# New places for the pieces of layer 0's front in a pass of a Mamba and mixture-of-experts kernel

## The chip, the cores and the metric

One Trainium2 chip, one core. The metric is the device time of one execution in microseconds. The program ran three times; the number to predict is the median of such runs for the changed kernel.

## The reference, cut to what matters

Two layers stand one after the other. The change lies in layer 0, which adds a Mamba block and a mixture of eight experts to its input (8192 tokens of 128 channels, 32 sequences of 256):

```python
xn = _layernorm(x)
x = x + mamba(xn) + moe(xn)
# mamba
xi, z = split(rmsnorm(xn) @ in_proj)
xi = silu(conv(xi) + conv_b)                      # 4 taps along a sequence
dt, Bm, Cm = split(xi @ x_proj)
delta = softplus(dt @ dt_w + dt_b)
h = exp(delta * A) * h + delta * xi * Bm          # along a sequence, 16 states
y = (sum_s(h * Cm) + xi * D) * silu(z)
mamba = y @ out_proj
# moe
probs = softmax(xn @ Wr + br)                     # 8 experts
gate = probs * keep                               # keep: sorted sum below 0.8
moe = sum_e(gate_e * (relu(xn @ W1_e + b1_e) @ W2_e + b2_e))
```

Layer 1 (attention and a capacity-bound mixture) isn't touched.

## The kernel before, in words

`layer0` walks through the tokens in 16 passes of 512 (`T0`). One pass has two kinds of work. The first is the body: 32 tiles of the scan (2 halves of the 256 inner channels, 4 groups of 4 states, 4 blocks of 32 channels) and eight experts. The second is the front of the next pass: everything from its input to delta, dx, z and the gate. The engines meet only through semaphores, so the order on each engine is the one written here.

A pass is divided into 32 half slots, h = 0 to 31. In each half slot the body does the same on every engine:
- ScalarE makes `dA` for tile h + 2, an exponential (`make_da`, L604). There are three banks for `dA`, so it waits for the product of tile h - 1 on VectorE.
- VectorE scans tile h in place (`scan`, L915) and multiplies it with C into `PR` (`times_c`, L925).
- GpSimd makes `dBx` for two tiles in every even half slot (`make_dbx`, L742) into one of two buffers. In half slots 2, 6, 10 and so on it adds an expert's result to `FF` (`accumulate`, L752).
- TensorE does two `up` products of an expert (L409) in half slots 0 and 1 of every four, and eight `down` products (L418) in each of half slots 2 and 3. The two `UP` banks are freed by ScalarE's relus (L613), two in each half slot that has `up` products. After the `down` products ScalarE multiplies by the gate (`apply_gate`, L620) in half slot 3 of every four. In half slots 1, 9, 17 and 25 TensorE folds 8 tiles of `PR` into `YS` (L431).

Into this the function `fore` puts the pieces of the front of the next pass, and `slot` puts the end of the pass before. One table for each engine says at which half slot a piece stands, behind the body's work of that half slot (`PE_AT`, `ACT_AT`, `DVE_AT`, `POOL_AT`, `SP_AT`, L204 to L211); a negative number means that many half slots before the pass. `pipeline` (L217) runs the two in turn. The pieces that the text below names, with their engine:
- `xproj` (TensorE, L499), `dt0` and `dt1` (TensorE, L508), read by ScalarE in `d0` and `d1` (L649, L650), which write `umax` and `soft`.
- the softplus: `exp` (ScalarE, L690), `one` (ScalarE, L694, adds 1 into `one_w`), `soft` (VectorE, L991), `ln` (ScalarE, L698, with a table load ahead and one behind), `lnw` (VectorE, L1001), `r` (GpSimd, L808), `delta` (GpSimd, L812), and `dx` = delta times xi (GpSimd, L819).
- `xi` (VectorE, L987), the convolved and gated input.
- the gate: `logits` (TensorE), `lg`, `gexp`, `gate1`, `rank` (GpSimd, five instructions from L829), `gate2`, `keep` (GpSimd, five instructions from L844), `gt` (TensorE and ScalarE, its transposition).
- `z0` and `z1` (TensorE, ScalarE's tanh, VectorE), and the products of y with them, `yz0` and `yz1` (GpSimd, L758).
- `out` (TensorE, L440 and L443): the output product of the pass before, added to `FF` and stored by `store` on VectorE (L939).
- `xm`, `xq`, `xs`, `ff` (GpSimd): the normalised inputs; `xnt`, `xqt` (TensorE): their transpositions.

All products of the front use one PSUM bank, `FRO`, in turn. SyncE's queue stores delta at `dst` and dx at `est`; behind `est` it issues the loads for the next pass's first half in this order: delta, dx (`load_delta`, `load_dx`), and at `bc0` a group of B and C (`load_states`). They go through DRAM to be spread over partitions: `dA` of the next pass needs the first, its `dBx` the other two. The other half follows in half slot 0.

Of the kernel before, what the change touches and what calls it, by code (L numbers as in the profile page):

```python
# [51 lines left out]
def layer0(nc, ctx, t, dram, scratch):  # L52
# [325 lines left out]
    def _(pe):  # L378
        for s in (front, upf, downf, sumf, outf):
            pe.sem_inc(s.sem, 2 * s.per)  # L380
# [72 lines left out]
        def slot(h, it, par, first=False, final=False, last_front=False):  # L453
# [4 lines left out]
            else:  # L458
# [3 lines left out]
                if half == 1 and s % 4 == 0:  # L462
                    if s:
                        add_states(s // 4 - 1, it)
                    elif not first:
                        add_states(HALF * NQ // 2 - 1, it - 1)
            if h == PE_AT["out"] and not first:
                if final:
                    output(it - 1, 1 - par, lambda: pe.wait_ge(gT_copied.sem, gT_copied.at(it, 1)))
# [1448 lines left out]
```

## Time and profile before

| | |
|---|---|
| median of 3 runs | 2114.2 us (2113.77 to 2116.78) |
| the profiled execution | 2115.22 us |
| its span, first to last instruction | 2113.4 us |
| layer 0: first scan to last store | about 76 to 1430 us |
| busy, of the span | PE 89%, DVE 79%, ACT 63%, POOL 62% |
| mean granted TensorE clock | 0.95 of full speed |

In this profile PE is TensorE, DVE is VectorE, ACT is ScalarE, POOL is GpSimd, and SPq is SyncE's DMA queue; PEld is the load of weights into TensorE. A row of a timeline gives the start in us from the span's beginning, the duration, the engine, the line, the operation with its tiles, and in brackets how long the engine had been idle and what ended that. A busy share is an average over layer 0 and layer 1, which have different limits.

### The profile page before, as it was taken

What the parts mean: (1) busy time and instruction counts of PE and PEld (TensorE: products, weight loads), DVE (VectorE), ACT (ScalarE), POOL (GpSimd) and SP (SyncE); (2) the same over time, 40 slices, a digit from 0 to 9 for tenths busy, and PEclk for the clock granted to TensorE, in tenths of its full rate; (3) what the DMA queues carried; (4) which work ended last, traced back from release to release, by engine and by line L of the source; (5) the groups of instructions that cost most, each with busy time, mean ns of one, the idle gap of its engine ahead of it and who ended that gap; (6) DMA issues with size and microseconds to landing.
All of it is one profiled execution on the core that took longest, in us unless ns stands there. A gap on an engine that the chain in (4) does not pass through costs nothing. (4 is left out here: it accounts for less than half of the span.)

```text
span 2113.4 us, 41732 instructions
## 1 busy us (share of the span) xinstructions
PE 1885.2 (89%) x14386; PEld 1156.0 (55%) x14386; DVE 1678.9 (79%) x2731; ACT 1337.2 (63%) x2423; POOL 1309.8 (62%) x1008
## 2 busy tenths in 40 slices
PE   4789998899998998999899999994899999998984
PEld 3356555565565655555556556553455555554542
DVE  5589888798898987988879889884888777886655
ACT  3587776776766767767577677651355555554653
POOL 2477877877878778688687787863333333333750
PEclk7899999999999999999999999995799999998997
DMA  8633615426346064263442633606444444455658
GB/s 188 164 80 78 140 48 117 100 52 141 77 87 139 28 137 100 53 140 76 88 112 50 135 87 67 140 6 168 118 114 119 116 117 117 117 136 138 171 149 244
DMA packets 212029, 235.27 MB, mean 111 GB/s; under 512 B 31590, under 2 KB 150414, under 8 KB 207694
## 3 DMA queue, kind: packets, MB, share of 16 engines
q1 hardware_dynamic: 207132, 227.99, 44.2%
q0 software_dynamic: 2048, 4.18, 0.7%
q8 instruction: 126, 2.06, 0.4%
q14 instruction: 99, 0.81, 0.1%
q10 hardware_dynamic: 2624, 0.23, 0.1%
HBM read 165.51 MB, written 66.85 MB: 110 GB/s over the span
## 5 line engine op out<-in xcount | busy, mean ns | idle before, releaser
L742 POOL TENSOR_TENSOR dBx<-REP,BC 128x1024 f32<-128x1024 f32 x256 | 604.1, 2362 | 231.7 <-DVE dA L915 191.6
L915 DVE TENSOR_TENSOR_SCAN dA<-dA,dBx 128x512 f32<-128x512 f32 x512 | 626.2, 1223 | 146.8 <-POOL dBx L742 125.5
L409 PE MATMUL UP<-xnT,W 128*128 128x512 f32 x1024 | 518.9, 623 | 60.1 <-ACT hT L613 45.9
L418 PEld LDWEIGHTS DN<-W,hT 128*128 128x128 f32 x4096 | 488.2, 196 | 77.6 <-issue 72.6
L418 PE MATMUL DN<-W,hT 128*128 128x128 f32 x4096 | 501.0, 281 | 1.3 <-ACT GD L620 1.3
L604 ACT ACTIVATE dA<-REP,A 128x512 f32<-128x512 f32 x512 | 355.0, 697 | 125.2 <-DVE PR L925 116.5
L613 ACT ACTIVATE hT<-UP,b 128x512 f32<-128x512 f32 x512 | 356.1, 695 | 57.5 <-PE UP L409 44.8
L925 DVE TENSOR_TENSOR PR<-dA,BC 128x512 f32<-128x512 f32 x512 | 353.2, 690 | 25.9 <-DVE dA L915 11.9
L409 PEld LDWEIGHTS UP<-xnT,W 128*128 128x128 f32 x1024 | 178.9, 193 | 294.6 <-ACT hT L613 174.4
L1820 DVE TENSOR_REDUCE NM<-S 128x4 f32<-128x1024 f32 (+1 forms) x192 | 233.8, 1218 | 78.3 <-PE S L1365 78.1
L1579 ACT ACTIVATE PT<-S 128x1024 f32<-128x1024 f32 x192 | 197.1, 1026 | 94.2 <-PE S L1365 94.2
L620 ACT ACTIVATE GD<-DN,gate 128x128 f32<-128x128 f32 x512 | 145.0, 365 | 93.4 <-PE DN L418 91.9
L752 POOL TENSOR_TENSOR FF<-FF,GD 128x512 f32<-128x512 f32 x128 | 163.4, 1277 | 6.9 <-ACT GD L620 6.9
L1633 POOL TENSOR_TENSOR t<-t 128x512 f32<-128x512 f32 x32 | 40.7, 1271 | 139.2 <-DVE t L1744 139.1
L431 PE MATMUL YS<-PR,fold 128*32 128x512 f32 x1024 | 124.0, 602 | 0.5 <-DVE PR L925 0.5
L1560 ACT COPY CS<-ACC 128x256 f32<-128x256 f32 x64 | 23.8, 372 | 104.3 <-PE ACC L1477 104.3
L1421 PE MATMUL OT<-PT,V 128*9 128x256 f32 x1024 | 84.2, 390 | 5.3 <-ACT PT L1579 5.2
L1639 POOL TENSOR_TENSOR SPL<-t,SPL 128x512 bf16<-128x512 f32 x32 | 37.1, 1158 | 72.6 <-ACT SPL L1585 72.5
L982 DVE SCALAR_TENSOR_TENSOR xch<-FRO,convw,xch 128x510 f32<-128x510 f32 (+2 forms) x93 | 69.1, 743 | 8.6 <-ACT xch L663 6.4
L431 PEld LDWEIGHTS YS<-PR,fold 128*32 128x32 f32 x1024 | 26.8, 110 | 89.1 <-issue 80.8
L1573 ACT COPY OSB<-OT 128x512 f32<-128x512 f32 x64 | 37.5, 585 | 59.2 <-PE OT L1423 59.2
L808 POOL TENSOR_TENSOR xch<-xch,soft 128x1024 f32<-128x1024 f32 x16 | 37.6, 2351 | 44.9 <-DVE soft L991 44.9
(254 smaller groups left out, 2662.7 us busy)
## 6 DMA issues: line engine op xcount, KB each, us to landing
BC<-s_b SPq DMA_DIRECT2D x128, 256.0 KB, 6.4
REP<-s_dx SPq DMA_DIRECT2D x124, 256.0 KB, 7.7
REP<-s_delta SPq DMA_DIRECT2D x124, 256.0 KB, 9.2
s_parts<-SPL SPq DMA_DIRECT2D x64, 192.0 KB
KS<-s_parts SPq DMA_DIRECT2D x64, 192.0 KB
QS<-s_parts SPq DMA_DIRECT2D x64, 192.0 KB
s_dx<-tz SPq DMA_DIRECT2D x16, 512.0 KB, 3.2
s_y<-zeros SPq DMA_DIRECT2D x32, 256.0 KB, 2.9
```

The costliest lines, as they stand in the source:

```text
L409: nc.tensor.matmul(UP[k % 2][:], W1[:, e % E0, f * P:(f + 1) * P], xnT[:, q, :], start=True, stop=True).then_inc(upf.sem, 1)
L418: last = nc.tensor.matmul(DN[:, j * P:(j + 1) * P], hT[:, e % 2, f, j * P:(j + 1) * P], W2[:, e, f, :], start=(f == 0), stop=(f == FB - 1))
L431: last = nc.tensor.matmul(YS[CB * j:CB * j + CB, :], fold[:], PR[:, DB * PLACE[b] + j, :], start=(b % NQ == 0), stop=(b % NQ == NQ - 1), t ...
L604: nc.scalar.activation(dA[:, k % 3, :], DR[:, h, j, :], ACT.Exp, scale=A[:, h, j, q:q + 1]).then_inc(da_ready.sem, 1)
L613: nc.scalar.activation(hT[:, e % 2, f, :], UP[k % 2][:], ACT.Relu, bias=b1[:, e % E0, f:f + 1]).then_inc(relu_done.sem, 1)
L620: last = nc.scalar.activation(GD[:, e % 2, j, :], DN[:, j * P:(j + 1) * P], ACT.Copy, scale=gate[:, par, j, e:e + 1])
L742: nc.gpsimd.tensor_tensor(dBx[:, s % 2], DX[:, h, j:j + 2, :], BC[:, q // 2, q % 2, :].unsqueeze(1).to_broadcast([P, 2, T0]), ALU.mult).th ...
L752: nc.gpsimd.tensor_tensor(FF[:, par], FF[:, par], GD[:, e % 2], ALU.add).then_inc(acc_done.sem, 1)
L915: nc.vector.tensor_tensor_scan(h, h, dBx[:, k // 2 % 2, k % 2, :], 0.0, ALU.mult, ALU.add).then_inc(scan_done.sem, 1)
L925: nc.vector.tensor_tensor(PR[:, DB * PLACE[b] + k % DB, :], dA[:, k % 3, :], BC[:, q // 2, 2 + q % 2, :], ALU.mult).then_inc(prod_done.sem, 1)
L1579: nc.scalar.activation(PT[:, u // 3, u % 3, :], S2[:].rearrange("p b w -> p (b w)"), ACT.Exp, scale=SCALE).then_inc(exp_done.sem, 1)
L1820: nc.vector.tensor_reduce(NM[:, 0 if a == 0 else 1, :].rearrange("p (r i) -> p r i", r=2)[:, :, heads], S1[:].rearrange("p r (j k) -> p r ...
```

## The change

The five tables get new numbers, so most pieces of the front stand at other half slots. Beside that:
- The output product `out` moves from half slot 8 to 16, where `ln` stands on ScalarE now, and `store` from 9 to 18; the transposition of the gate, `gt`, goes from the front into the body of its own pass, half slot 8.
- Adding the one, a ScalarE activation before, is a `tensor_scalar` on VectorE (`w`, half slot 15).
- z of the first half has two buffers, like z of the second; tanh writes straight into them, where before it went through `xch`. So `yz0` can stand in the following pass (half slot 8).
- In half slots with `up` products ScalarE does both relus ahead of its `dA`; they stood around it.
- SyncE's load of the next input moves from half slot 12 to 20, the store of the result from 10 to 19.

Where the instructions stand now, at three places. **ScalarE around the exponential of the softplus** (`soft<-soft` is `exp`, `tz<-soft` is `one`, `GD` the gating, `hT` a relu). Before:

```order
L604 ACTIVATE dA<-REP,A 128x512
L620 ACTIVATE GD<-DN,gate 128x128 x4
L613 ACTIVATE hT<-UP,b 128x512
L604 ACTIVATE dA<-REP,A 128x512
L613 ACTIVATE hT<-UP,b 128x512
L649 ACTIVATE xch<-FRO,dtb 128x512
L650 ACTIVATE soft<-FRO,dtb 128x512
L613 ACTIVATE hT<-UP,b 128x512
L604 ACTIVATE dA<-REP,A 128x512
L613 ACTIVATE hT<-UP,b 128x512
L690 ACTIVATE soft<-soft 128x1024
L694 ACTIVATE tz<-soft 128x1024
```

and now:

```order
L608 ACTIVATE dA<-REP,A 128x512
L659 ACTIVATE xch<-FRO,dtb 128x512
L660 ACTIVATE soft<-FRO,dtb 128x512
L608 ACTIVATE dA<-REP,A 128x512
L659 ACTIVATE xch<-FRO,dtb 128x512
L660 ACTIVATE soft<-FRO,dtb 128x512
L608 ACTIVATE dA<-REP,A 128x512
L626 ACTIVATE GD<-DN,gate 128x128 x4
L700 ACTIVATE soft<-soft 128x1024
L617 ACTIVATE hT<-UP,b 128x512 x2
L608 ACTIVATE dA<-REP,A 128x512
L704 ACT_TABLE_LOAD
```

The exponential stood two relus, `d1` and two more relus behind the gating of half slot 15 and is now directly behind it; `d1` has moved ahead of that gating, and `one` is gone.

**GpSimd from r to dx** (`xch<-xch,soft` is r, `soft<-xch,th` is delta, `tz<-soft,xi` is dx, `y` a product with z, `FF<-FF,GD` an expert's addition, `FF<-XN,XI` is `ff`). Before:

```order
L808 TENSOR_TENSOR xch<-xch,soft 128x1024
L812 TENSOR_TENSOR soft<-xch,th 128x1024
L815 TENSOR_TENSOR lg<-lg,g 128x32
L742 TENSOR_TENSOR dBx<-REP,BC 128x1024
L752 TENSOR_TENSOR FF<-FF,GD 128x512
L758 TENSOR_TENSOR y<-y,z 128x512
L819 TENSOR_TENSOR tz<-soft,xi 128x1024
```

and now:

```order
L810 TENSOR_TENSOR xch<-xch,soft 128x1024
L744 TENSOR_TENSOR dBx<-REP,BC 128x1024
L754 TENSOR_TENSOR FF<-FF,GD 128x512
L806 TENSOR_TENSOR FF<-XN,XI 128x512
L744 TENSOR_TENSOR dBx<-REP,BC 128x1024
L814 TENSOR_TENSOR soft<-xch,th 128x1024
L744 TENSOR_TENSOR dBx<-REP,BC 128x1024
L754 TENSOR_TENSOR FF<-FF,GD 128x512
L821 TENSOR_TENSOR tz<-soft,xi 128x1024
```

Two more `dBx`, one more addition and `ff` stand between r and dx; the product with z and lg have left.

**GpSimd at the end of a pass** (`cum`, `cnt` and `gate` are `keep`; the `dBx` ahead of an `FF` is the next pass's first). Before:

```order
L752 TENSOR_TENSOR FF<-FF,GD 128x512
L844 TENSOR_SCALAR cum<-cum 128x32
L845 TENSOR_SCALAR cnt<-cnt 128x32
L847 TENSOR_TENSOR cum<-cum,cnt 128x32
L849 TENSOR_TENSOR cum<-cum,pr 128x32
L851 TENSOR_TENSOR gate<-pr,cum 128x32
L742 TENSOR_TENSOR dBx<-REP,BC 128x1024
L795 TENSOR_TENSOR XQ<-XN,q 128x512
L799 TENSOR_TENSOR XN<-XN,rstd 128x512
L742 TENSOR_TENSOR dBx<-REP,BC 128x1024
L752 TENSOR_TENSOR FF<-FF,GD 128x512
```

and now:

```order
L744 TENSOR_TENSOR dBx<-REP,BC 128x1024
L754 TENSOR_TENSOR FF<-FF,GD 128x512
L846 TENSOR_SCALAR cum<-cum 128x32
L847 TENSOR_SCALAR cnt<-cnt 128x32
L849 TENSOR_TENSOR cum<-cum,cnt 128x32
L851 TENSOR_TENSOR cum<-cum,pr 128x32
L853 TENSOR_TENSOR gate<-pr,cum 128x32
L744 TENSOR_TENSOR dBx<-REP,BC 128x1024
L801 TENSOR_TENSOR XN<-XN,rstd 128x512
L744 TENSOR_TENSOR dBx<-REP,BC 128x1024
```

`keep` stood two `dBx` earlier and stands now behind the next pass's first `dBx` and the addition.

The diff, cut to its core:

```diff
-    umax, lnw, one_w, tanhz = xch, th, tz, xch
+    umax, lnw, one_w = xch, th, tz
...
-z0 = sb("z0", [P, T0])
+z0 = sb("z0", [P, 2, T0])
...
-    PE_AT = dict(xqt=-2, x0=0, x1=4, out=8, xproj=10, dt0=12, dt1=16, xnt=17, logits=19, z0=23, z1=27, gt=29)
-    ACT_AT = dict(xr=-2, tap0=2, tap1=4, tanh=6, dtb=10, d0=14, d1=16, xn=18, exp=17, one=17, ln=18, gexp=20, tz0=23, tz1=27, gt=29)
-    DVE_AT = dict(conv0=3, conv1=5, xi=8, soft=19, lg=19, lnw=20, gate1=23, z0=25, gate2=27, z1=29, ev1=3, store=9, stat=12, ev0=21)
-    POOL_AT = dict(xm=-7, xq=-4, xs=-4, ff=10, r=20, dx=23, rank=23, yz1=3, yz0=22, delta=20, lg=21, keep=27)
+    PE_AT = dict(xqt=-4, x0=0, x1=4, gt=8, xproj=10, dt0=12, dt1=14, out=16, z0=19, xnt=21, logits=23, z1=25)
+    ACT_AT = dict(xr=-3, tap0=1, tap1=4, tanh=6, gt=8, dtb=10, d0=13, d1=14, exp=15, ln=16, tz0=20, xn=21, gexp=26, tz1=26)
+    DVE_AT = dict(conv0=2, ev1=3, conv1=5, xi=8, w=15, soft=16, store=18, lnw=18, z0=20, ev0=21, lg=24, z1=26, gate1=27, stat=28, gate2=30)
+    POOL_AT = dict(xm=-7, xq=-6, xs=1, yz0=8, yz1=12, r=17, ff=19, delta=20, dx=22, lg=25, rank=28, keep=31)
...
-    SP_AT = dict(bst=11, dst=15, est=23, bc0=26, save=10, load=12)
+    SP_AT = dict(bst=11, dst=20, est=23, bc0=26, save=19, load=20)
...
+            if h == PE_AT["gt"]:
+                pe.wait_ge(gate_made.sem, gate_made.at(it, 5))
+                pe.wait_ge(z_done.sem, z_done.at(it, 2))
+                if not final:
+                    pe.wait_ge(conv_step.sem, conv_step.at(it + 1, 6))
+                nc.tensor.transpose(FRO[:, 0:P], gate_all[:, par, :], ident[:]).then_inc(gtf.sem, 1)
...
             if ups:
                 relu(s // 2 + 1, it, 2 * half)
+                relu(s // 2 + 1, it, 2 * half + 1)
             if not (final and s == SLOTS - 1):
                 make_da(h + 2, it)
-            if ups:
-                relu(s // 2 + 1, it, 2 * half + 1)
...
-            if h == ACT_AT["one"]:
-                act.wait_ge(sp_done.sem, sp_done.at(n, 1))
-                act.wait_ge(e_stored.sem, e_stored.at(n - 1, 16))
-                nc.scalar.activation(one_w[:], soft[:], ACT.Identity, bias=1.0).then_inc(sp_done.sem, 1)
...
-                    nc.scalar.activation(tanhz[:, k, :], bank(n, k)[:], ACT.Tanh, scale=0.5).then_inc(tanh_z.sem, 1)
+                    z = (z0, z1)[k][:, q, :]
+                    act.wait_ge(yz_done.sem, yz_done.at(n - 2, k + 1))
+                    act.wait_ge(front.sem, front.at(n, (7, 10)[k]))
+                    nc.scalar.activation(z, bank(n, k)[:], ACT.Tanh, scale=0.5).then_inc(tanh_z.sem, 1)
...
-            if h == POOL_AT["yz1"] and not first:
-                times_z(1, it - 1, 1 - par)
-            if h == POOL_AT["yz0"]:
-                times_z(0, it, par)
+            for k in range(HALF):
+                if h == POOL_AT[f"yz{k}"] and not first:
+                    times_z(k, it - 1, 1 - par)
...
+            if h == DVE_AT["w"]:
+                dve.wait_ge(sp_done.sem, sp_done.at(n, 1))
+                dve.wait_ge(e_stored.sem, e_stored.at(n - 1, 16))
+                nc.vector.tensor_scalar(one_w[:], soft[:], 1.0, None, ALU.add).then_inc(w_done.sem, 1)
```

The other lines follow from the new order: semaphores that count the pieces, and waits that name the piece which now stands ahead in `FRO`.

## Rows read from the trace of the kernel before

**Rows 1.** SyncE's queue over time: start us, us, line, operation, idle before.

```profile
227.32 0.39 SPq L362 DMA_DIRECT2D s_dx<-tz  x1
...
991.06 0.38 SPq L362 DMA_DIRECT2D s_dx<-tz  x1
...
1249.36 0.38 SPq L362 DMA_DIRECT2D s_dx<-tz  x1
```

**Rows 2.** VectorE over time: the start's `soft`, then one pass.

```profile
43.66 1.22 DVE L991 SCALAR_TENSOR_TENSOR soft<-tz,soft 128x1024 f32<-128x1024 f32 x1 [0.41 <-ACT tz L694]
...
928.08 1.23 DVE L915 TENSOR_TENSOR_SCAN dA<-dA,dBx 128x512 f32<-128x512 f32 x1 [1.60 <-POOL dBx L742]
...
930.15 1.22 DVE L915 TENSOR_TENSOR_SCAN dA<-dA,dBx 128x512 f32<-128x512 f32 x1
...
932.01 1.22 DVE L915 TENSOR_TENSOR_SCAN dA<-dA,dBx 128x512 f32<-128x512 f32 x1
...
965.70 1.22 DVE L915 TENSOR_TENSOR_SCAN dA<-dA,dBx 128x512 f32<-128x512 f32 x1
...
974.37 2.13 DVE L991 SCALAR_TENSOR_TENSOR soft<-tz,soft 128x1024 f32<-128x1024 f32 x1 [0.69 <-ACT tz L694]
...
996.92 1.23 DVE L915 TENSOR_TENSOR_SCAN dA<-dA,dBx 128x512 f32<-128x512 f32 x1 [4.83 <-POOL dBx L742]
...
1012.16 1.23 DVE L915 TENSOR_TENSOR_SCAN dA<-dA,dBx 128x512 f32<-128x512 f32 x1 [2.56 <-POOL dBx L742]
```

**Rows 3.** GpSimd over time in the same pass.

```profile
973.03 2.38 POOL L742 TENSOR_TENSOR dBx<-REP,BC 128x1024 f32<-128x1024 f32 x1 [0.56 <-DVE dA L915]
976.57 2.35 POOL L808 TENSOR_TENSOR xch<-xch,soft 128x1024 f32<-128x1024 f32 x1 [1.16 <-DVE soft L991]
...
1001.59 0.29 POOL L844 TENSOR_SCALAR cum<-cum 128x32 f32<-128x32 f32 x1
...
1003.08 2.36 POOL L742 TENSOR_TENSOR dBx<-REP,BC 128x1024 f32<-128x1024 f32 x1
...
1009.52 2.36 POOL L742 TENSOR_TENSOR dBx<-REP,BC 128x1024 f32<-128x1024 f32 x1 [1.80 <-DMA BC<-s_b]
1011.84 1.26 POOL L752 TENSOR_TENSOR FF<-FF,GD 128x512 f32<-128x512 f32 x1
```

**Rows 4.** Stretches: us, busy of PE, PEld, DVE, ACT, POOL, clock, DMA, GB/s.

```profile
996.50:1001.50 5.00, 5.00 (x32) 3.64 (x30) 4.51 (x7) 2.59 (x7) 4.94 (x4) 1.00 1.08 220
...
976.50:991.03 14.53, 12.37 (x57) 7.84 (x55) 13.05 (x18) 11.25 (x23) 11.99 (x8) 0.88 0.10 37
```

**Rows 5.** Waits from 188 to 1267 us: in total, times, longest.

```profile
POOL dBx L742 <- DMA BC<-s_b: 18.3, 11, 2.2
```

**Rows 6.** ScalarE over time in the same pass.

```profile
946.54 0.69 ACT L604 ACTIVATE dA<-REP,A 128x512 f32<-128x512 f32 x1 [0.81 <-DVE PR L925]
...
948.16 0.70 ACT L613 ACTIVATE hT<-UP,b 128x512 f32<-128x512 f32 x1
...
966.47 1.14 ACT L620 ACTIVATE GD<-DN,gate 128x128 f32<-128x128 f32 x4 [0.21 <-PE DN L418]
...
972.13 1.12 ACT L690 ACTIVATE soft<-soft 128x1024 f32<-128x1024 f32 x1
```

**Rows 7.** TensorE over time in the same pass.

```profile
949.25 1.98 PE L409 MATMUL UP<-xnT,W 128*128 128x512 f32 x4
...
966.27 1.88 PE L409 MATMUL UP<-xnT,W 128*128 128x512 f32 x4
967.99 1.02 PE L508 MATMUL FRO<-dtB,dtw 128*128 128x512 f32 x2
...
981.49 3.26 PE L409 MATMUL UP<-xnT,W 128*128 128x512 f32 x4 [2.14 <-ACT hT L613]
```

**Rows 8.** Groups by form on VectorE: busy us, mean ns, idle before.

```profile
L904 DVE TENSOR_SCALAR inproj<-inproj,rmsw 128x512 f32<-128x512 f32 x1 | 0.5, 481 | 0.0
```

More of the change, by code:

```diff
@@ L113, in layer0 @@
     FRO = ctx.enter_context(nc.psum_tensor("FRO", [P, 512], F32))
-    front = signal("front", 11)
+    front = signal("front", 10); gtf = signal("gtf", 1)
     upf = signal("upf", E0 * FB); downf = signal("downf", E0); sumf = signal("sumf", HALF * NQ // 2); outf = signal("outf", 1)
@@ L353, in fore @@
                 if start:
-                    load_x(1)
                     load_states(0, n, q)
@@ L359, in fore @@
                     sp.dma_start(seqs(d_d[q][k * P:(k + 1) * P, :])[:, :, 1:], seqs(delta[:, k, :])[:, :, 1:]).then_inc(d_stored.sem, 16)
+                if start:
+                    load_x(1)
             elif h == SP_AT["est"]:
@@ L378, in _ @@
     def _(pe):
-        for s in (front, upf, downf, sumf, outf):
+        for s in (front, gtf, upf, downf, sumf, outf):
             pe.sem_inc(s.sem, 2 * s.per)
@@ L470, in slot @@
                 else:
-                    output(it - 1, 1 - par, lambda: pe.wait_ge(conv_step.sem, conv_step.at(it + 1, 6)))
+                    output(it - 1, 1 - par, lambda: pe.wait_ge(u_done.sem, u_done.at(it + 1, 2)))
         def fore(h, n, q):
@@ L684, in fore @@
                 act.wait_ge(upf.sem, upf.at(n - 2, E0 * FB))
-                act.wait_ge(front.sem, front.at(n, 7))
+                act.wait_ge(front.sem, front.at(n, 8))
                 nc.scalar.copy(xnT[:, q, :], FRO[:]).then_inc(xT_copied.sem, 1)
@@ L785, in fore @@
                     pool.wait_ge(stat_step2, 21)
-                pool.wait_ge(front.sem, front.at(n - 1, 7))
+                pool.wait_ge(front.sem, front.at(n - 1, 8))
                 pool.wait_ge(xi_loaded.sem, xi_loaded.at(n, 16))
@@ L856, in _ @@
     def _(dve):
-        for s in (conv_step, gate_step, z_done, xi_done, log_step, scan_done, prod_done, ev_done, x_done, restat):
+        for s in (conv_step, gate_step, z_done, xi_done, w_done, log_step, scan_done, prod_done, ev_done, x_done, restat):
             dve.sem_inc(s.sem, 2 * s.per)
@@ L987, in fore @@
                 nc.vector.scalar_tensor_tensor(xi[:, q], th[:], 1.0, xch[:], ALU.add, ALU.mult).then_inc(xi_done.sem, 1)
+            if h == DVE_AT["w"]:
+                dve.wait_ge(sp_done.sem, sp_done.at(n, 1))
+                dve.wait_ge(e_stored.sem, e_stored.at(n - 1, 16))
+                nc.vector.tensor_scalar(one_w[:], soft[:], 1.0, None, ALU.add).then_inc(w_done.sem, 1)
             if h == DVE_AT["soft"]:
-                dve.wait_ge(sp_done.sem, sp_done.at(n, 2))
+                dve.wait_ge(w_done.sem, w_done.at(n, 1))
                 nc.vector.scalar_tensor_tensor(soft[:], one_w[:], -1.0, soft[:], ALU.add, ALU.subtract).then_inc(log_step.sem, 1)
-            if h == (DVE_AT["lnw"] + 1 if isinstance(n, int) and n == 0 else DVE_AT["lg"]):
-                dve.wait_ge(front.sem, front.at(n, 8))
+            if h == DVE_AT["lg"]:
+                dve.wait_ge(front.sem, front.at(n, 9))
                 gstep(nc.vector.tensor_tensor(lg[:], FRO[:, 0:J0 * E0].rearrange("p (j e) -> p j e", e=E0),
```

47 lines of the change are left out of this document (21 added, 26 removed).

## The prediction, made before the changed kernel ran

> **What bounds the kernel now.** Layer 0 is sixteen passes over 512 tokens, and the change touches only these, so I first looked for what repeats in every pass. The DMA queue's timeline gives the period: the store of dx is issued at 227.32 us and, twelve passes later, at 1249.36 us [rows 1], so a pass takes 85.2 us on average. I then read one pass, from the first scan at 928.08 to the next pass's first scan at 1012.16 [rows 2], 84.1 us, on one engine after the other. All times t below count from 928.08.
>
> The pass closes in a ring, and I cut it in three. **A**, from the first scan (half slot 0) to the moment GpSimd starts r, that is, when VectorE has written `soft`: 976.57 [rows 3], t = 48.5. **B**, from r to the end of dx, when its store is issued: 991.06 [rows 1], 14.5 us. **C**, from there to the next first scan: 21.1 us. In C the SyncE queue stores dx and then loads half of delta, half of dx and a group of B and C, 3 MB in all, and the DMA engines are full (share 1.08, 220 GB/s [rows 4]). The product dBx of the next pass waits for the last of it, 1.80 us at 1009.52 [rows 3], and the scan for that product, 2.56 us [rows 2]. The list of waits has this DMA wait in 11 of the passes between 188 and 1267 us [rows 5]. So C is a transfer that nothing in the change shortens; the period is A + B + C, and what counts is how early dx ends.
>
> The view that misleads is the largest single stall, 4.83 us of VectorE at 996.92 behind dBx [rows 2], where r, delta, dx and the ranking stand close together on GpSimd. It lies inside C. If it goes, VectorE reaches the end of the pass earlier and waits there for the same transfer.
>
> **The change, part by part.** *In C.* The ranking leaves the place behind dx. The stall of 4.83 us goes, and I cost that at nothing: the 3 MB hide it, and the first scan is late next. The gate's last five instructions (1.49 us, 1001.59 to 1003.08 [rows 3]) now stand behind the dBx that waits for the transfer, together with the addition that stood there. From the end of that dBx to the end of the next one it was addition and product, and it will be 1.25 + 1.49 + 2.32 = 5.05 us (2.32 is 1009.52 to 1011.84 [rows 3]). The scan of half slot 2 stood at t = 3.93 [rows 2]; it will stand at about 5.08. Term: VectorE 1.15 us later.
>
> *In A, TensorE and ScalarE.* The output product leaves half slot 8, so TensorE gets there early, but the next `up` products need the relus of half slot 8. ScalarE does those behind a dA that waits for VectorE (0.81 us at 946.54) and behind a gating; the first relu started at 948.16 [rows 6] and ended at t = 20.8. With the 1.15 us above, TensorE starts half slot 9 at t = 21.9; before, behind the output product, it started at 949.25 [rows 7], t = 21.2. Taking the output product away gains nothing here. From there to the end of half slot 15 it needed 17.0 us (to 966.27 [rows 7]). Into this stretch comes the second delta product, 0.9 us (row 967.99 [rows 7]), which waits for the reading of the first; that reading is four ScalarE instructions behind the second `up` product of half slot 13, and I put the wait at 0.7 us, between 0 and 1.1. So half slot 15 ends at 21.9 + 17.0 + 0.9 + 0.7 = 40.5. The exponential stands behind the gating of just that half slot: 1.2 us (966.27 to the end of 966.47's group [rows 6, 7]) and 1.1 us (row 972.13 [rows 6]) give 42.8.
>
> *In A, VectorE.* The new addition of one waits for that exponential. VectorE came to the end of half slot 15 at 965.70, t = 37.6 [rows 2]; with 1.15 and the 1.1 below it would be 39.9 at the latest, and less, since store and statistics have left. So it waits about 3 us, with all scans queued behind it, and the transfer does not hide this since it is ahead of dx. No row shows this operation at 1024 columns. From below it is 0.48 us (512 columns [rows 8]), from above 1.22 us (1024 columns, two inputs [rows 2]); I take 0.8, near the smaller row's rate. Then one slot (1.86 us, 930.15 to 932.01) and `soft` at 1.2 us: 42.8 + 0.8 + 1.86 + 1.2 = 46.7. ScalarE's own addition of one and the relus that stood ahead of its exponential are gone from this path: A falls from 48.5 to 46.7.
>
> *The port.* `soft` took 1.22 us at 43.66 and 2.13 us at 974.37 [rows 2]. In the second case a product had started on GpSimd at 973.03 and took 2.38 [rows 3], so it ended at 975.41, and VectorE's instruction ended 1.1 us after that: it had waited for it. Its sisters xi and lnw, which have two inputs in SBUF as well, met no GpSimd instruction before. Now xi stands behind GpSimd's product with z, which moved to half slot 8, and lnw behind a product or an addition: 1.1 us each (a whole instruction shared between them, 0 to 2.4). xi's is off TensorE's path to the exponential, so it adds nothing; lnw's delays delta. The Trainium skill ("GPSIMD Engine Reference", section "Specifications") states more than this row: the interfaces to SBUF are shared with VectorE instructions that have two SBUF inputs or run in a two-port mode. The new addition of one would be of the second kind; no row has such an instruction beside GpSimd, and by the page it could wait too. In my sum it comes when GpSimd has nothing to do, so neither reading changes it; without any port wait B would be 1.1 us shorter and the time 2135.
>
> *In B.* Before, GpSimd did r, delta, the small lg, one dBx, one addition, the product with z, and dx. Now it does r, dBx, addition, FF, dBx, delta, dBx, addition, dx: six instructions of 1024 columns at 2.32 us (13.9), three of 512 at 1.25 (3.75), and lnw's port wait (1.1): 18.75 us for 14.5. GpSimd is never idle in it, so this is the sum of a queue.
>
> *The rest.* z in two buffers lets the product with z move; the wait it removes was not on the ring. The input load and the result's store move up on SyncE's queue to just before delta's store, 0.5 MB that is gone before C begins. The end of the last pass gets one more product with z on GpSimd, beside TensorE's last fold: 0 to 1.25 us, I take 0. The start has its pieces in a chain anyway: 0, at most 1 either way.
>
> **Sum.** A + B was 48.5 + 14.5 = 63.0 and becomes 46.7 + 18.75 = 65.45: 2.45 us per pass, 15 passes with a front: +37 us. The profiled execution took 2115.2 us, 1 us over the median; on the median of 2114.2 this gives **2151 us**. With the bounds of the waits (0.4 and 1.1 less, or 1.3 more) this case lies between 2128 and 2171.
>
> **The rivals.** *Even.* The exponential is not late: TensorE gets to half slot 15 sooner than my 40.5. Then VectorE is held there only by the port: dBx starts behind the scan of half slot 15 and holds the addition for some 1.7 us: product and its start lie 2.4 us behind the scan, the multiplication between 0.7. From about 38.5 (39.9 less the two instructions that left, my estimate) A is 38.5 + 1.7 + 0.8 + 1.86 + 1.2 = 44, A + B 62.75, the time 2110. For it: TensorE could lead more, since both relus now stand before the dA. Against: the relus of half slot 8 still stand behind a dA.
>
> *Faster.* This decides if in addition GpSimd is through with the gate before half slot 2 and the port is free when VectorE comes: A = 44 - 1.15 - 1.1 = 41.75, B = 17.65, 3.6 us less per pass, 2060. It needs TensorE to end half slot 15 before t = 36. For it speaks that every engine's work is spread more evenly; against it, that three waits must all be wrong.
>
> *Slower still.* TensorE waits some 4 us before half slot 9, longer than any wait of this pass. At 981.49, after 2.14 us of waiting, four matmuls took 3.26 us [rows 7], against 1.98 at 949.25, and the granted clock of that stretch was 0.88 [rows 4], so some of it ran at the lower level, 1.2 GHz. That is 1.3 us in those four alone; with what ran behind them I take 2 us per pass, all on the way to the exponential: +30, 2181.
>
> **How the numbers follow.** My case 0.55, even 0.13, faster 0.20, slower still 0.12. A measurement of this kernel can tell about 0.2%, 4 us, from no change. Faster by more than that: the faster rival and 0.05 of the even one, 0.25. Within it: 0.07. Slower: 0.68. The range from 2088 to 2185 leaves out half of the faster rival and a little of the slowest, some 0.15.
>
> **What would show it.** The store of dx some 2.5 us later in the pass; VectorE idle for 3 us before the new TENSOR_SCALAR, released by ScalarE's exponential; VectorE idle about 1 us before the scan of half slot 2; GpSimd without a gap from r to dx, 18 to 19 us; the stall behind the ranking gone and the wait for BC's transfer longer, 3 to 5 us; lnw and xi at over 2 us in the rows by form. I am wrong if the store of dx comes earlier than t = 62, or if C is not 21 us but shrinks with the work in it.

## The result, and the profile after

The change makes the kernel slower: 2164.6 us (median of 4 runs, 2162.6 to 2168.2) against 2115.5 us (2113.8 to 2118.1) for the kernel before on the same chip, a ratio of 1.0253 with a 95% interval of 1.0219 to 1.0287. The profiled execution took 2165.9 us, its span is 2164.1 us, 50.7 us longer than the span of before.

The same views, in the order of the prediction. SyncE's queue first (start us, us, line, operation), the rows that answer to [rows 1]:

```profile
228.97 0.38 SPq L363 DMA_DIRECT2D s_dx<-tz  x1
...
939.27 0.37 SPq L363 DMA_DIRECT2D s_dx<-tz  x1
1029.79 0.37 SPq L363 DMA_DIRECT2D s_dx<-tz  x1
1116.98 0.37 SPq L363 DMA_DIRECT2D s_dx<-tz  x1
1207.27 0.37 SPq L363 DMA_DIRECT2D s_dx<-tz  x1
1296.45 0.37 SPq L363 DMA_DIRECT2D s_dx<-tz  x1
```

The period is (1296.45 - 228.97) / 12 = 89.0 us on average, 85.2 before. Read the neighbours too: 90.5, 87.2, 90.3, 89.2. The passes are not alike, and the sum of the forecast had only one kind.

VectorE over one pass (in brackets the idle time before, and what ended it), the rows that answer to [rows 2]:

```profile
961.06 1.23 DVE L917 TENSOR_TENSOR_SCAN dA<-dA,dBx 128x512 f32<-128x512 f32 x1 [5.21 <-POOL dBx L744]
...
966.09 1.23 DVE L917 TENSOR_TENSOR_SCAN dA<-dA,dBx 128x512 f32<-128x512 f32 x1 [1.02 <-POOL dBx L744]
...
984.25 2.23 DVE L989 SCALAR_TENSOR_TENSOR xi<-th,xch 128x1024 f32<-128x1024 f32 x1
...
1007.34 0.69 DVE L994 TENSOR_SCALAR tz<-soft 128x1024 f32<-128x1024 f32 x1 [4.40 <-ACT soft L700]
1007.95 1.23 DVE L917 TENSOR_TENSOR_SCAN dA<-dA,dBx 128x512 f32<-128x512 f32 x1
1009.21 0.69 DVE L927 TENSOR_TENSOR PR<-dA,BC 128x512 f32<-128x512 f32 x1
1009.82 1.22 DVE L998 SCALAR_TENSOR_TENSOR soft<-tz,soft 128x1024 f32<-128x1024 f32 x1
```

The scan of half slot 2 stands at 966.09 - 961.06 = 5.03 (3.93 before), behind `keep`; VectorE waits 4.40 us for the exponential, then needs 0.69 us for the addition of one; the stall of 4.83 us behind the ranking is gone, and 5.21 us of waiting stand before the first scan instead of 2.56.

GpSimd from r to dx, in the next pass, the rows that answer to [rows 3]:

```profile
1098.31 2.38 POOL L810 TENSOR_TENSOR xch<-xch,soft 128x1024 f32<-128x1024 f32 x1 [6.46 <-DVE soft L998]
1100.65 2.36 POOL L744 TENSOR_TENSOR dBx<-REP,BC 128x1024 f32<-128x1024 f32 x1
1102.98 2.25 POOL L754 TENSOR_TENSOR FF<-FF,GD 128x512 f32<-128x512 f32 x1
1105.18 1.29 POOL L806 TENSOR_TENSOR FF<-XN,XI 128x512 f32<-128x512 f32 x1
1106.43 2.36 POOL L744 TENSOR_TENSOR dBx<-REP,BC 128x1024 f32<-128x1024 f32 x1
1108.74 2.36 POOL L814 TENSOR_TENSOR soft<-xch,th 128x1024 f32<-128x1024 f32 x1
1111.06 2.37 POOL L744 TENSOR_TENSOR dBx<-REP,BC 128x1024 f32<-128x1024 f32 x1
1113.37 1.28 POOL L754 TENSOR_TENSOR FF<-FF,GD 128x512 f32<-128x512 f32 x1
1114.59 2.37 POOL L821 TENSOR_TENSOR tz<-soft,xi 128x1024 f32<-128x1024 f32 x1
```

No gap from 1098.31 to 1116.96: B = 18.65 us, 14.46 before. GpSimd's wait for BC's transfer from 188 to 1267 us (in total, times, longest), the row that answers to [rows 5]:

```profile
POOL dBx L744 <- DMA BC<-s_b: 60.0, 12, 5.6
```

TensorE around half slot 9 in the same two passes, and then the view by stretches (length, busy time of PE, PEld, DVE, ACT and POOL, granted clock, DMA share, GB/s) of the seven us behind each start:

```profile
978.80 0.33 PE L474 MATMUL FRO<-ident,gate 128*128 128x128 f32 x1 [0.34 <-DVE xch L984]
983.02 3.78 PE L410 MATMUL UP<-xnT,W 128*128 128x512 f32 x4 [3.89 <-ACT hT L617]
986.73 3.13 PE L432 MATMUL YS<-PR,fold 128*32 128x512 f32 x16
...
1073.22 1.98 PE L410 MATMUL UP<-xnT,W 128*128 128x512 f32 x4 [1.78 <-ACT hT L617]
1075.14 1.92 PE L432 MATMUL YS<-PR,fold 128*32 128x512 f32 x16
```

```profile
983.00:990.00 7.00, 6.98 (x21) 1.98 (x22) 6.90 (x7) 3.97 (x7) 4.70 (x3) 0.56 0.01 2
1073.20:1080.20 7.00, 6.98 (x40) 3.58 (x41) 6.90 (x7) 3.87 (x7) 4.70 (x3) 1.00 0.00 0
```

After a wait of 3.89 us the granted clock is 0.56 of full speed, so most of that stretch ran at 1.2 GHz; after one of 1.78 us it is 1.00, all at 2.4 GHz. The same four `up` products and sixteen folds take 6.9 us in the one pass and 3.9 in the other.

With the same cuts as in the prediction, means in us over the 14 passes that start between 159 and 1350 us (A from the first scan to the start of r, B to the end of dx, C to the next first scan, and VectorE's idle time before that scan), for these two kernels and all that follow:

| kernel | A | B | C | idle before next first scan | ratio to before, 95% |
|---|---|---|---|---|---|
| before | 49.71 | 14.42 | 20.78 | 2.2 | 1 |
| the change | 48.81 | 18.65 | 21.35 | 4.6 | 1.0253 (1.0219 to 1.0287) |
| gate transposed twenty times | 47.21 | 18.66 | 21.61 | 4.9 | 1.0177 (1.0138 to 1.0216) |
| ranking and `keep` earlier | 47.37 | 18.65 | 21.10 | 3.3 | 1.0131 (1.0092 to 1.0170) |
| addition of one later, dx at 24 | 49.93 | 19.08 | 21.57 | 7.1 | 1.0393 (1.0351 to 1.0435) |
| addition of one later, dx at 22 | 50.47 | 16.06 | 21.21 | 3.8 | 1.0178 (1.0135 to 1.0220) |
| before, with dx at 24 | 49.59 | 16.75 | 20.56 | 4.8 | 1.0154 (1.0114 to 1.0195) |
| before, with the ranking at 28 | 51.80 | 14.42 | 20.62 | 2.9 | 1.0085 (1.0059 to 1.0111) |
| half of dx's first load left out | 48.09 | 18.66 | 18.38 | 1.6 | 1.0021 (0.9999 to 1.0043) |
| `keep` earlier, delta and dx earlier | 47.64 | 15.12 | 22.24 | 0.9 | 0.9992 (0.9970 to 1.0015) |
| the same, addition of one at 16 | 47.61 | 15.11 | 22.28 | 0.9 | 0.9996 (0.9980 to 1.0012) |
| the same, and r at 18 | 49.97 | 11.84 | 22.51 | 0.9 | 0.9941 (0.9920 to 0.9961) |

For the change against before: A 0.90 us shorter, B 4.23 longer, C 0.57 longer, +3.9 us per pass. These 14 passes make +54.7 us (1406.59 - 163.22 for 1353.02 - 164.34); the change is 1.1 us ahead where they begin, and takes 2.9 us less from their end to the end of the program: together 50.7, the difference of the spans.

### The profile page after: what moved, and what is told of

The parts are those of the page before. It is cut to its first block and busy times, and to the rows that moved or that the text cites. A ratio compares the mean times of both kernels' runs of the same rounds, so it can differ in the third digit from the quotient of the medians.

```text
span 2164.1 us, 41725 instructions
## 1 busy us (share of the span) xinstructions
PE 1889.2 (87%) x14386; PEld 1152.7 (53%) x14386; DVE 1698.7 (78%) x2747; ACT 1337.1 (62%) x2407; POOL 1321.7 (61%) x1008
## 5 line engine op out<-in xcount | busy, mean ns | idle before, releaser
L419 PEld LDWEIGHTS DN<-W,hT 128*128 128x128 f32 x4096 | 477.1, 192 | 89.1 <-issue 87.4
L419 PE MATMUL DN<-W,hT 128*128 128x128 f32 x4096 | 487.9, 276 | 1.3 <-ACT GD L626 1.3
L617 ACT ACTIVATE hT<-UP,b 128x512 f32<-128x512 f32 x512 | 342.6, 692 | 78.8 <-PE UP L410 71.2
L410 PEld LDWEIGHTS UP<-xnT,W 128*128 128x128 f32 x1024 | 185.4, 200 | 291.4 <-issue 147.5
L754 POOL TENSOR_TENSOR FF<-FF,GD 128x512 f32<-128x512 f32 x128 | 177.5, 1387 | 5.6 <-ACT GD L626 5.6
L432 PE MATMUL YS<-PR,fold 128*32 128x512 f32 x1024 | 131.1, 632 | 0.9 <-DVE PR L927 0.9
L1565 ACT COPY CS<-ACC 128x256 f32<-128x256 f32 x64 | 23.8, 372 | 104.0 <-PE ACC L1482 104.0
```

The lines of the kernel that those rows point to most:

```text
L410: nc.tensor.matmul(UP[k % 2][:], W1[:, e % E0, f * P:(f + 1) * P], xnT[:, q, :], start=True, stop=True).then_inc(upf.sem, 1)
L419: last = nc.tensor.matmul(DN[:, j * P:(j + 1) * P], hT[:, e % 2, f, j * P:(j + 1) * P], W2[:, e, f, :], start=(f == 0), stop=(f == FB - 1))
L432: last = nc.tensor.matmul(YS[CB * j:CB * j + CB, :], fold[:], PR[:, DB * PLACE[b] + j, :], start=(b % NQ == 0), stop=(b % NQ == NQ - 1), t ...
L617: nc.scalar.activation(hT[:, e % 2, f, :], UP[k % 2][:], ACT.Relu, bias=b1[:, e % E0, f:f + 1]).then_inc(relu_done.sem, 1)
L754: nc.gpsimd.tensor_tensor(FF[:, par], FF[:, par], GD[:, e % 2], ALU.add).then_inc(acc_done.sem, 1)
```

## The experiments

Four theories stood against each other. **The ring**: A + B + C as forecast, VectorE's waits within it cost nothing. **The hold**: VectorE's new wait of 4.4 us at the addition of one, with all scans queued behind it, is the loss. **The clock**: TensorE's lower clock behind its wait before half slot 9. **The stall**: the large stall of before, behind the ranking, was worth its size.

### The hold taken away, with two places for dx

```diff
-    DVE_AT = dict(..., w=15, soft=16, store=18, lnw=18, ...)
-    POOL_AT = dict(..., r=17, ff=19, delta=20, dx=22, ...)
+    DVE_AT = dict(..., w=17, soft=18, store=18, lnw=19, ...)
+    POOL_AT = dict(..., r=18, ff=19, delta=20, dx=24, ...)
```

(dx stays at 22 in the second kernel.)

> VectorE's addition of one stands two half slots later (17), soft at 18, lnw at 19, GpSimd's r at 18 and dx at 24, so VectorE does two more slots while the exponential is made, and is not held. Ring theory (A + B + C; VectorE's hold of 4.4 us at the addition costs nothing by itself): A stays, since it is the exponential's end (t about 44), the addition 0.8, a slot 1.86 and soft 1.2; B on GpSimd is r, ff, dBx, delta, dBx, addition, dBx, dx = 2.38 + 1.29 + 2.36 + 2.36 + 2.37 + 1.28 + 2.37 + 2.37 = 16.8 us for 18.65; C stays: 1.9 us less in each of 15 passes, 2137 us. Rival, the hold is the cost: 4.4 us less in each pass beside it, 2071 us at the least change of B, and VectorE's idle time before the first scan not longer than 5 us. By the ring this idle time grows by the hold, to 8 or 9 us.

> The same with dx at 22, one product dBx earlier on GpSimd. Ring theory: B is 14.4 us, 4.2 us less than in the changed kernel and 2.4 less than with dx at 24; 2102 us, and 36 us between the two kernels, as long as C stays at 21 us. Rival, the hold is the cost: dx's place makes no difference, both kernels give the same time within 5 us. A third possibility, that VectorE's or GpSimd's own work becomes the bound in C: the difference between the two is under 36 us, and the wait of dBx for the transfer is gone.

Measured: 2196.0 us with dx at 24, 2153.8 with dx at 22. The hold is gone (VectorE waits 0.15 us for the exponential, below), and the first of the two kernels is yet slower than the change: taking the hold away is worth less than what came with it. One product between r and dx is worth 42 us by the runs, 3.0 us of B; the ring had 36. But both lie over 50 us above the ring's numbers, and the reason is in the rows of the kernel with dx at 22. VectorE, then GpSimd:

```profile
907.61 2.12 DVE L994 TENSOR_SCALAR tz<-soft 128x1024 f32<-128x1024 f32 x1 [0.15 <-ACT soft L700]
...
911.97 1.21 DVE L998 SCALAR_TENSOR_TENSOR soft<-tz,soft 128x1024 f32<-128x1024 f32 x1
914.79 1.23 DVE L917 TENSOR_TENSOR_SCAN dA<-dA,dBx 128x512 f32<-128x512 f32 x1 [1.62 <-ACT dA L608]
916.06 0.69 DVE L927 TENSOR_TENSOR PR<-dA,BC 128x512 f32<-128x512 f32 x1
916.67 1.28 DVE L1008 SCALAR_TENSOR_TENSOR th<-tz,th 128x1024 f32<-128x1024 f32 x1
```

```profile
906.81 2.37 POOL L744 TENSOR_TENSOR dBx<-REP,BC 128x1024 f32<-128x1024 f32 x1 [1.88 <-DVE dA L917]
...
916.83 3.34 POOL L744 TENSOR_TENSOR dBx<-REP,BC 128x1024 f32<-128x1024 f32 x1
920.12 2.36 POOL L814 TENSOR_TENSOR soft<-xch,th 128x1024 f32<-128x1024 f32 x1
923.41 2.36 POOL L744 TENSOR_TENSOR dBx<-REP,BC 128x1024 f32<-128x1024 f32 x1 [0.93 <-DVE dA L917]
```

The addition of one (L994) took 0.69 us in the change, with GpSimd idle, and takes 2.12 here: a product runs on GpSimd from 906.81 to 909.18, and the addition ends at 909.73, 0.55 us behind it. So this operation waits for a running GpSimd instruction too, which the prediction had left open. It goes the other way as well: `lnw` starts at 916.67, and the product that starts at 916.83 takes 3.34 us instead of 2.36. The Trainium skill says so in "SBUF — State Buffer", section "SBUF: two separate sides": of a GpSimd instruction and a VectorE instruction that runs in a two-port mode, or has two SBUF inputs while the GpSimd instruction reads SBUF, the one that starts first keeps the shared ports for its whole length, and the other blocks. The rows agree in both directions: 2.12 us for 0.69 where GpSimd started first, 3.34 for 2.36 where VectorE did.

So A grew by 1.1 to 1.7 us in these kernels. VectorE's last scan now ends just ahead of the exponential, and GpSimd's product starts behind that scan: 1.43 us of port wait, and beside it the store, which now stands between the addition and `soft`. B is 1.7 us (dx at 22) and 2.3 us (dx at 24) over its sum, for the same reason and one more: 0.98 us of the longer product, 0.93 for a scan of VectorE, which is late by now, and with dx at 24 another 0.64 for the next. With dx at 24 VectorE idles 7.1 us before the next first scan, 4.6 in the change: part of the time that it is not held, it waits there. So the hold itself costs nothing here (a run below that takes 1.9 us of it away gains nothing either), and it even kept that port wait out of A.

### The clock

```diff
-                nc.tensor.transpose(FRO[:, 0:P], gate_all[:, par, :], ident[:]).then_inc(gtf.sem, 1)
+                for _ in range(20):
+                    last = nc.tensor.transpose(FRO[:, 0:P], gate_all[:, par, :], ident[:])
+                last.then_inc(gtf.sem, 1)
```

> TensorE repeats the transposition of the gate twenty times in half slot 8, some 2 us inside the 3.9 us that it waits there in every second pass; it writes the same values. Clock theory (in those passes the four up products of half slot 9 took 3.78 us instead of 1.98 and the exponential ended 2.2 us later): the up products take 1.98 in all passes, the seven or eight slow passes lose 2.2 us each, 2148 us. Rival, the two kinds of pass come from the loop's code (two passes to a round) and not from the clock: no gain, 2163 to 2168 us, the up products still at 3.78.

Measured: 2152.1 us, the ratio falls from 1.0253 to 1.0177, by 16 us at 2114. TensorE of this kernel, in a pass whose first scan stands at 954.07, and the view by stretches of its half slot 9:

```profile
971.83 2.40 PE L475 MATMUL FRO<-ident,gate 128*128 128x128 f32 x20 [0.34 <-DVE xch L986]
976.05 1.99 PE L410 MATMUL UP<-xnT,W 128*128 128x512 f32 x4 [1.82 <-ACT hT L619]
977.96 1.92 PE L432 MATMUL YS<-PR,fold 128*32 128x512 f32 x16
```

```profile
976.07:983.07 7.00, 7.00 (x40) 3.61 (x41) 6.90 (x7) 3.82 (x7) 4.70 (x4) 1.00 0.00 0
```

TensorE starts half slot 9 at the same t = 22.0, after 2.40 us of useless work and 1.82 of waiting, and stays at full clock. A is between 46.8 and 48.1 in all 14 passes, where it was between 47.1 and 50.1. The clock theory is shown, at about the size that it claimed (2148 us). It is not the whole: the kernel is still 1.8% above before. C grew by 0.26 us, in five of the passes by over 1 us, each of them the second pass of a round of the loop; why stays open.

The length of the wait alone doesn't decide it. In the kernel with the late addition and dx at 22, the clock is lower behind a wait of 1.90 us in one pass; in the kernel with less to transfer (below), it is full behind one of 3.35 us. Their stretches from the start of half slot 9:

```profile
709.33:716.33 7.00, 7.00 (x34) 2.93 (x35) 6.90 (x7) 3.86 (x7) 4.70 (x3) 0.76 0.00 0
1119.66:1126.66 7.00, 7.00 (x40) 3.60 (x41) 6.90 (x7) 3.85 (x7) 4.70 (x4) 1.00 0.01 2
```

### `keep` ahead of the product that waits

```diff
-    DVE_AT = dict(..., stat=28, gate2=30)
-    POOL_AT = dict(..., rank=28, keep=31)
+    DVE_AT = dict(..., stat=28, gate2=29)
+    POOL_AT = dict(..., rank=27, keep=29)
```

> The ranking moves to half slot 27, gate2 and keep to 29, so that keep stands ahead of the product dBx that waits for the transfer and no more behind it. Ring theory: VectorE's wait of 1.0 to 1.25 us before the scan of half slot 2 goes, A is 1.0 us shorter in 15 passes, 2149 us; and if TensorE's wait before half slot 9 gets shorter by as much, up to 2 us more in some passes. Rival, the relus of half slot 8 are bound elsewhere (taps, convolution): no change, 2163 to 2166 us, the exponential's end still at t = 43.9 or 46.1.

Measured: 2142.4 us, a ratio of 1.0131 for 1.0253, some 26 us at 2114. A fell by 1.44 us, more than the 1.0 expected: TensorE starts half slot 9 at t = 20.5 to 20.9 in nine of the 14 passes, where it was 21.8 to 22.0 in nine, and its four `up` products took over 2.8 us in seven passes instead of nine. So the wait that the change put in front of half slot 2 did reach the exponential.

### One more product ahead of dx, in the kernel before

```diff
-    POOL_AT = dict(..., r=20, dx=23, rank=23, ...)
+    POOL_AT = dict(..., r=20, dx=24, rank=24, ...)
```

> The kernel before with one number changed twice: GpSimd's dx stands at half slot 24 instead of 23, and the ranking behind it at 24, so that one more product dBx stands between r and dx, and one half slot's product comes earlier for VectorE. Ring theory: B grows by one product, 14.45 to 16.8 us, A and C stay, +2.35 us in 15 passes, 2150 us, although VectorE's stall behind the ranking gets shorter. Rival, VectorE's stall of 4.8 us behind dx and the ranking is what costs: 2.4 us less per pass, 2080 us.

Measured: 2146.7 us, +33 us by the ratio. B is 16.75 us, 2.33 more; A and C are 0.1 and 0.2 less; and VectorE has its product earlier and idles 4.8 us before the first scan. This is the plainest sign of the ring: one product of 2.36 us, which now stands ahead of dx, gives the loss of 33 us in 14 passes. The ranking moved along with dx, and VectorE's earlier product saved nothing.

### The stall behind the ranking, in the kernel before

```diff
-    PE_AT = dict(..., gt=29)
-    ACT_AT = dict(..., gt=29)
-    DVE_AT = dict(..., gate2=27, ...)
-    POOL_AT = dict(..., rank=23, ..., keep=27)
+    PE_AT = dict(..., gt=30)
+    ACT_AT = dict(..., gt=30)
+    DVE_AT = dict(..., gate2=29, ...)
+    POOL_AT = dict(..., rank=28, ..., keep=29)
```

> The kernel before with the ranking at half slot 28 (it stood at 23, straight behind dx), gate2 and keep at 29, and the gate's transposition at 30. VectorE's stall of 4.83 us goes. Ring theory: it lies inside C, which is a transfer; VectorE then waits some 7 us before the first scan instead of 2.6, and the time stays within 6 us of the kernel before, 2109 to 2121 us. Rival, the stall is on the path: 4.8 us less in 15 passes, 2042 us.

Measured: 2133.0 us, a ratio of 1.0085: no gain, and a loss that neither theory had. VectorE's idle times in one C of this kernel (the middle row is `gate2`):

```profile
1015.71 1.23 DVE L915 TENSOR_TENSOR_SCAN dA<-dA,dBx 128x512 f32<-128x512 f32 x1 [1.33 <-POOL dBx L742]
...
1026.10 0.42 DVE L1015 TENSOR_REDUCE cnt<-gt 128x32 f32<-128x256 f32 x1 [2.69 <-POOL eq L839]
...
1033.77 1.23 DVE L915 TENSOR_TENSOR_SCAN dA<-dA,dBx 128x512 f32<-128x512 f32 x1 [2.59 <-POOL dBx L742]
```

The stall was not taken away but split: 1.33 us at its old place, and 2.69 where `gate2` now waits for the ranking. So the run doesn't separate the two theories well. What does is the change itself: there the stall is gone, VectorE idles 4.6 us before the first scan for 2.2, and C is no shorter (21.35 for 20.78). C is the same here too, 20.62; the loss is in A, 51.80, where in three of the 14 passes ScalarE shows a gap of 5.6 to 6.4 us at the loop's edge that no wait explains (before has two, of 3.4 and 5.5). The rest of A's growth I did not settle.

### Less to transfer in C

```diff
-        def load_rep(rep, src, h, loaded):
+        def load_rep(rep, src, h, loaded, blocks=DB):
...
-                sp.dma_start(rep[CB * r:CB * r + CB, h, :, :], rows).then_inc(loaded[h].sem, 16)
+                sp.dma_start(rep[CB * r:CB * r + CB, h, 0:blocks, :], rows[:, 0:blocks, :]).then_inc(loaded[h].sem, 16)
...
-            load_rep(DX, e_d[q], h, dx_loaded)
+            load_rep(DX, e_d[q], h, dx_loaded, DB // 2 if h == 0 else DB)
```

> The changed kernel, in which each pass after the first loads only two of the four blocks of 32 channels of dx for its first half: four loads of 128 KB instead of 256 KB; the other two blocks hold the values of the first pass. Half a MB less of the 3 MB that are moved between the end of dx and the first scan. Theory, C is the transfer: at the 220 GB/s that these engines moved, 2.3 us less in each pass, 2131 us, and VectorE's idle time before the first scan falls from 5 to under 3 us. Rival, C is the work in it (VectorE's and GpSimd's, which end 5 us before) or a fixed cost of each load: no change, 2163 to 2166 us.

Measured: 2117.3 us, 47 us less than the change (1.0021 for 1.0253 gives 49). C is 18.38, 2.97 us less, and VectorE's idle time before the first scan fell to 1.6 us. So C is the transfer, and half a MB of its 3 weighs more than the 2.3 us that the mean rate gave. Not all of the 47 us is C's: A is 0.72 us shorter too, since the four `up` products of half slot 9 took over 2.8 us in seven passes instead of nine.

### Putting dx back, in the change

```diff
-    POOL_AT = dict(..., delta=20, dx=22, ...)
+    POOL_AT = dict(..., delta=18, dx=20, ...)
```

on top of the kernel with the early ranking and `keep`.

> The kernel with the early ranking and keep (2142 us), and beside that GpSimd's delta at 18 and dx at 20, so that one product dBx, one addition and one more dBx no longer stand between r and dx. B is then r, dBx, addition, delta, ff, dBx, dx = 2.38 + 2.36 + 1.3 to 2.25 + 2.36 + 1.29 + 2.36 + 2.37, 14.4 to 15.4 us for 18.65. Ring theory with C a pure transfer: 3.3 to 4.2 us less in 15 passes, 2080 to 2092 us. But the two products that VectorE needs for half slots 22 to 25 come 2.4 us later, and VectorE had 3.0 to 3.9 us to spare before the first scan: if this room is used up, the period is set by VectorE and GpSimd in C, and the gain is 1 to 2 us per pass, 2112 to 2127 us; I take this one. Rival, B does not count (a product late for VectorE counts): 2.4 us more per pass, 2178 us.

Measured: 2113.3 us, the time of before (0.9970 to 1.0015). B fell to 15.12, as worked out. The gain is 2.1 us per pass, since C is no longer a pure transfer: VectorE comes to the first scan without idle time, and GpSimd runs from r to the product for it without a gap worth the name. In five of the 14 passes, every second one between 331 and 1017 us, a gap like that of this row of VectorE is added:

```profile
846.69 1.23 DVE L917 TENSOR_TENSOR_SCAN dA<-dA,dBx 128x512 f32<-128x512 f32 x1 [2.56 <-issue]
```

It stands at the edge of the loop, which holds two passes. In the change such a gap fell on TensorE, while the ring waited for the transfer anyway (4.42 us at 1049.13, five of that kind in the span). With VectorE as the bound it counts: C is 23.8 to 24.0 us in the five passes that end there and 21.1 to 21.4 in the others.

### Using the hold

On top of the last kernel:

```diff
-    DVE_AT = dict(..., w=15, soft=16, ...)
+    DVE_AT = dict(..., w=16, soft=17, ...)
```

and in the second kernel `r=18` for `r=17` on GpSimd.

> The kernel with the early ranking and keep and the early delta and dx (2113 us), and VectorE's addition of one, soft one half slot later (16 and 17): VectorE does one slot more, 1.86 us, while the exponential is made, and its hold falls from 4.4 to 2.5 us. In that kernel VectorE itself set the first scan (no idle time before it, or 2.4 us at the loop's edge). Theory: A stays at 47.4, since the addition still meets no GpSimd product; from r to the first scan VectorE needs 1.86 us less, and the bound there is again B + C = 15.1 + 21.4 = 36.5 us, which GpSimd's row of work without a gap (34.1 us and a product of 2.35) also gives; it was 37.5 on average. 1 us less per pass, 2098 us. Rival, the hold costs nothing in any place: no change, 2108 to 2118 us; or the addition meets a product and takes 2.1 us: 2117 us.

> The same with r at 18, so that a product dBx and an addition stand ahead of r and are made while VectorE and ScalarE make soft. Theory: A grows by 1.8 us (product and addition after the scan of half slot 17, 4.9 us from the end of the addition of one to r for 3.06), and soft waits for the product on the port, 2 us for 1.22; B falls to r, delta, ff, dBx, dx, 10.8 to 11.3 us; VectorE then sets the first scan, some 34.7 us after r; the pass is 84 us, 2098 us. Rival: B + C alone counts, 49.3 + 11 + 21.4 = 81.7 us per pass, 2064 us.

Measured: 2112.2 us for the first, no change, as the rival had it. The hold fell to 2.54 us and what VectorE gained it lost elsewhere: it waits 2.29 us for ScalarE's tanh of z (at 989.21), 0.44 in the kernel above; C is the same, and the gap at the loop's edge stays. The second kernel takes 2104.1 us, a ratio of 0.9941 (0.9920 to 0.9961): faster than the change and, by 0.6%, than the kernel before; near the theory's 2098, and far from the 2064 of B + C alone. A grew by 2.4 us, of which 1.66 are `soft`: it met the product that stands ahead of r and took 2.88 us for 1.22. B fell by 3.3, to 11.84:

```profile
964.58 0.69 DVE L994 TENSOR_SCALAR tz<-soft 128x1024 f32<-128x1024 f32 x1 [2.54 <-ACT soft L700]
965.19 1.22 DVE L917 TENSOR_TENSOR_SCAN dA<-dA,dBx 128x512 f32<-128x512 f32 x1
966.45 0.69 DVE L927 TENSOR_TENSOR PR<-dA,BC 128x512 f32<-128x512 f32 x1
967.06 2.88 DVE L998 SCALAR_TENSOR_TENSOR soft<-tz,soft 128x1024 f32<-128x1024 f32 x1
```

## Why the prediction was right, and where its terms were off

**The direction and its cause.** Slower, through the ring, and B was the term: 18.75 us forecast, 18.65 measured, no gap on GpSimd. The change earns in A and pays more than that in B, and the large stall that it removes is worth nothing. The kernel before with dx one product later, and the change with delta and dx put back, show B from both sides.

**C and the stall.** Forecast: C stays at 21.1, the wait for BC's transfer grows to 3 to 5 us. Measured: 21.35, and 12 waits of 60.0 us in all, up to 5.6; [rows 5] had 11 of 18.3. The run with half a MB less shows that it is the transfer. C came out 0.57 us above the mean of before, some 8 us over the passes, and the cause of this part of the miss stays open. One guess doesn't account for it: VectorE ends the pass earlier, so SyncE issues the next group's loads of B and C 16.5 to 17.1 us behind the end of dx, 18.5 to 18.7 before, while the transfer still runs. In the kernel before with dx at 24 they stand even earlier, at 14.9 to 16.1 us, and its C is 0.2 us shorter than before.

**`keep`.** The scan of half slot 2 at t = 5.08 forecast, 5.03 measured; TensorE at half slot 9 at 21.9, measured 21.8 to 22.0 in nine of the 14 passes. The path through the relus held, as the run with the early `keep` shows.

**The exponential.** Forecast at t = 42.8; measured 43.2 to 44.0 in the five passes without a slow half slot 9, and what follows it (addition 0.69, a slot, `soft` 1.22) is as forecast: A was 47.6 in these, for 46.7. This is the term of the sum that came out wrong by most, 0.9 us. The wait of the second delta product was 0.76 us for 0.7, the product itself 1.12 for 0.9; in three of the five TensorE also started half slot 9 at 22.7 to 22.8, in one at 22.3. VectorE's wait was 4.4 us for 3, which changes nothing.

**The clock.** What failed here is the separation of my case from the rival "slower still". I had given that 0.12, with its price as 2 us per pass. It was true in nine of the 14 passes and false in five: A is 49.5 on average in the nine, 47.6 in the others, 1.9 us apart. So the mechanism and its price were right, and the chance was not one of all passes or none. My own sum could have said more of it: the output product left its place ahead of half slot 9, next to nothing came there, and half slot 9 was still to start at t = 21.9, so the time of that product had to become a wait. The kernel without the drops takes 2152.1 us, next to the 2151 of my case, but that closeness is partly luck: against the means of before its A is 2.5 us shorter, where I had 1.8, and its C 0.8 longer, where I had nothing.

**The reference pass.** The sum was taken against one clean pass of before (A + B = 63.0). The mean of before is 64.1, since some of its passes carry gaps at the loop's edge within A, like this one of ScalarE, in a pass with an A of 55.8:

```profile
1018.72 0.69 ACT L613 ACTIVATE hT<-UP,b 128x512 f32<-128x512 f32 x1 [5.51 <-issue]
```

Most of those of the change lie in C, where the transfer hides them. And I multiplied by 15, where 14 passes carry the loss: the first is 0.3 us shorter than before, and what stands behind the 14 takes 2.9 us less. By clean passes (the five of the change without a slow half slot 9, the six of before with an A of 48.5) the change costs A - 0.9 (47.6 for 48.5), B + 4.2, C + 0.7 (21.7 for 21.1): 4.0 us for my 2.45. By the means it is 3.9: the clock adds 1.2 to the A of the change (48.8 for 47.6), and the longer passes, most of them at the loop's edge, add 1.2 to that of before (49.7 for 48.5). So these two cancel, and what my sum lacked in the end is the 0.9 us at the exponential and the growth of C.

**The bounds.** Those of the case don't follow from its waits. A wait put at 0.7 between 0 and 1.1 gives 0.7 less or 0.4 more, one put at 1.1 between 0 and 2.4 gives 1.1 less or 1.3 more, so 2124 to 2177 instead of 2128 to 2171. The measured time lies in both.

**The port.** xi took 2.23 us as forecast. `lnw` was to take over 2 us and delay delta by 1.1; it took 1.77:

```profile
1102.33 1.77 DVE L1008 SCALAR_TENSOR_TENSOR th<-tz,th 128x1024 f32<-128x1024 f32 x1
```

The addition on GpSimd beside it, at 1102.98 in the rows above, paid more: 2.25 us, where the next one took 1.28. The sum of B was right with the wait in another row.

**The other rivals.** "Even" and "faster" needed an exponential that is not late; VectorE's wait for it, 4.3 to 4.4 us in each of the 14 passes, rules them out.

## What to carry to other kernels

Cut a pass into the ring that closes it before pricing an edit: a wait of 4 us that lies beside a transfer was worth nothing here, and one product moved ahead of the instruction which starts this transfer cost its full length in each pass. A piece of work taken from an engine leaves a wait behind; where this is TensorE, look at the granted clock of what follows, for it was the useless work in that gap that gave back 16 us. And take the mean pass, not the cleanest, as the thing that is compared.

## What the runs showed of the hardware

A VectorE addition of a constant in float32, 128 x 1024, takes 0.69 us alone and 2.12 us when it meets a GpSimd product that has started; one with two inputs in SBUF took 2.13 and 2.88 us instead of 1.22 beside such a product; and GpSimd's instruction pays instead when VectorE's has started first (3.34 us for 2.36). Half slot 9 of TensorE ran at a granted clock of 0.56 behind one wait and of 1.00 behind another or behind useless work in the wait's place, and the length of the wait (1.8 to 3.9 us) doesn't sort the two by itself. At the edge of the loop TensorE, ScalarE or VectorE, up to three of them in one round, stand still for 1.3 to 7.3 us with no wait that the profile shows; whether this costs anything depends on what the ring waits for there.
